# Two fp16 parts per operand in the tree layer's products, its weights loaded and split ahead

## The reference

```python
logits = x @ W_in.T + b_in                       # 2048 x 2040
decisions = (logits > 0).astype(jnp.int32).reshape(B, PAR, N_NODES)
acts = jax.nn.silu(logits).reshape(B, PAR, N_NODES)
...
for d in range(DEPTH):                           # 7 levels: walk from node to node by the decisions
    moves = jnp.take_along_axis(decisions, current[..., None], axis=2)[..., 0]
    current = (current - cur_platform) * 2 + moves + next_platform
    dmap = dmap + jax.nn.one_hot(current, N_NODES, dtype=acts.dtype)
masked = acts * jax.lax.stop_gradient(dmap)
out = masked.reshape(B, WIDTH) @ W_out.T         # 2048 x 256
```

## Time and profile before

| | us |
|---|---|
| median of 3 runs | 3735.11 |
| lowest and highest run | 3732.72, 3735.58 |
| profiled execution | 3734.91 |
| its span, first to last instruction | 3733.2 |
| PE busy in the span | 3208.2 (86%) |
| DVE busy in the span | 2112.1 (57%) |

### The profile page before, as it was taken

One profiled execution on the slowest core, in us unless ns is written; L12 is line 12 of the kernel. 1 busy time (PEld: TensorE's weight loads), 2 busy tenths in 40 slices (PEclk: granted clock), 3 DMA queues, 4 the chain that ended last, 5 costly groups with the idle time before them and its releaser, 6 DMA issues. The chain is left out here.

```text
span 3733.2 us, 108642 instructions
## 1 busy us (share of the span) xinstructions
PE 3208.2 (86%) x44394; PEld 2109.9 (57%) x44394; DVE 2112.1 (57%) x8196; ACT 1495.3 (40%) x4199; POOL 642.8 (17%) x361
## 2 busy tenths in 40 slices
PE   7798575898989895679984788899999999999899
PEld 3323342222323222578972334599999899999566
DVE  6312554555555533666648444377777777777554
ACT  3465542455555540477843122222222222222222
POOL 0000000466666671151210000000000000000000
PEclk8779787999999996789987899755555555555999
DMA  1000003000000004211120000100000000000000
GB/s 69 1 1 12 0 1 112 1 1 1 1 1 1 1 1 143 102 47 55 50 94 0 26 0 0 57 4 4 4 4 4 5 4 4 4 4 4 6 8 9
DMA packets 53375, 79.42 MB, mean 21 GB/s; under 512 B 11878, under 2 KB 43323, under 8 KB 51996
## 3 DMA queue, kind: packets, MB, share of 16 engines
q1 hardware_dynamic: 47504, 61.59, 5.0%
q0 software_dynamic: 3408, 9.34, 0.7%
q10 hardware_dynamic: 1988, 1.77, 0.2%
HBM read 56.01 MB, written 16.67 MB: 19 GB/s over the span
## 5 line engine op out<-in xcount | busy, mean ns | idle before, releaser
L1308 DVE TENSOR_REDUCE diff_mx<-diff_m_ps 128x1 f32<-128x512 f32 x512 | 329.9, 686 | 330.2 <-PE diff_m_ps L1158 330.2
L2773 PE MATMUL gru_sums<-gru_take,gru_u 128*128 128x4 f16 x12288 | 479.8, 167 | 4.4 <-issue 3.7
L2773 PE MATMUL gru_sums<-gru_keep,gru_u 128*128 128x4 f16 x12288 | 471.3, 166 | 1.3
L2773 PEld LDWEIGHTS gru_sums<-gru_take,gru_u 128*128 128x128 f16 x12288 | 432.8, 105 | 4.7 <-issue 3.7
L2773 PEld LDWEIGHTS gru_sums<-gru_keep,gru_u 128*128 128x128 f16 x12288 | 410.8, 104 | 14.8 <-issue 1.5
L1262 ACT ACTIVATE diff_probs<-diff_s_ps 128x512 f32<-128x512 f32 x512 | 277.9, 595 | 225.0 <-PE diff_s_ps L1152 225.0
L1152 PE MATMUL diff_s_ps<-diff_qk 32*128 32x512 f32 x1024 | 294.9, 649 | 63.7 <-DVE diff_mx L1308 56.1
L2773 PE MATMUL gru_sums<-gru_rh,gru_u 128*128 128x4 f16 x6144 | 279.6, 170 | 27.5 <-DVE gru_rh L2842 4.6
L1158 PE MATMUL diff_m_ps<-diff_qk 32*128 32x512 f32 x1024 | 293.5, 650 | 6.4 <-DVE diff_mx L1308 6.4
L1354 POOL TENSOR_TENSOR diff_sums<-diff_sums,diff_probs 128x2048 f32<-128x2048 f32 x64 | 289.3, 4520 | 32.0 <-ACT diff_probs L1262 31.8
L2773 PEld LDWEIGHTS gru_sums<-gru_rh,gru_u 128*128 128x128 f16 x6144 | 237.3, 107 | 69.9 <-DVE gru_rh L2842 6.6
(11 more groups left out here) (486 smaller groups left out, 5660.1 us busy)
## 6 DMA issues: line engine op xcount, KB each, us to landing
moe_weights<-in_L_ffn_W SPq DMA_DIRECT2D x16, 1024.0 KB, 13.0
expert_slots<-diff_blank SPq DMA_DIRECT2D x1, 5031.0 KB, 21.1
stream_a<-expert_slots SPq DMA_DIRECT2D x39, 129.0 KB, 2.1
moe_weights<-in_L_cond_w_R SPq DMA_DIRECT2D x1, 4096.0 KB, 14.8
moe_both<-expert_pairs SPq DMA_DIRECT2D x4, 1024.0 KB, 9.6
stream_b<-in_x SPq DMA_DIRECT2D x4, 512.0 KB, 8.1
hyp_wf<-in_L_cond_w_f SPq DMA_DIRECT2D x2, 1024.0 KB, 8.5
stream_b<-in_xT SPq DMA_DIRECT2D x1, 2048.0 KB, 12.5
```

Source lines behind the costliest of these rows:

```text
L1308: dve.tensor_reduce(mx[:, i % 2, kt, at:at + 1], m_ps[:, m % 3, :], X_AXIS, ALU.max).then_inc(ph.maxes_ready, 1)
L2773: last = pe.matmul(sums[:, par, g, m * B:(m + 1) * B], part[:, g, c, m * P:(m + 1) * P], state[:, c * B:(c + 1) * B], start=False, stop=(l ...
```

## The change

Both products of the tree are formed from two fp16 parts per operand: a first part (the value, scaled, rounded to fp16) and a second (what is left, in fp16). Three products stand for one: first x first, second x first and first x second.

- `linear_attention` now issues the tree's three loads too, behind the recurrence's eleven, on SP in its first block. The recurrence's preparation issues none.
- The recurrence's preparation finds the largest entries of the tree's weights and bias on DVE (three reductions), turns and spreads them through PE between the matmul groups n = 11 and n = 13, and derives scales. ACT forms the first parts of the weights in four pieces of 128 x 2048, behind its copies n = 15 to 18; DVE forms the second parts.
- The multiplication of `hist` by 1/SCALE at the end of the recurrence is gone.
- In the tree POOL makes the states' first part (fp16), copies the residual, copies the states whole, and subtracts for the second part.
- PE forms the logits from 24 fp16 matmuls of 512 columns, and the result from 48 fp16 matmuls of 256 columns. Its order within a tile: transposes 0 and 1, product 0, transposes 2, product 1, transposes 3, products 2 and 3.
- ACT copies each group of transposes out as the first part, scaled (`turn_first`); DVE then forms the second part from the same bank of PSUM and from the first part, and only this frees the bank and lets PE multiply (`turn_read`). So DVE has four more instructions per tile, behind the multiplication by the path and ahead of the next tile's bias.

```diff
--- before.py
+++ after.py
@@ linear_attention, first block, SP
-                next_weights.load(sp, io)
+                for weights in next_weights:
+                    weights.load(sp, io)
@@ recurrence, preparation, PE
+                        if n == 11:
+                            pe.wait_ge(ph.tree_found, 1)
+                            pe.transpose(pst[0:3, 6, 2 * P:3 * P], found[:, :], ident[:, :]).then_inc(ph.tree_turned, 1)
+                        if n == 13:
+                            pe.wait_ge(ph.tree_reduced, 1)
+                            pe.matmul(pst[:, 6, 3 * P:3 * P + 3], ones[0:3, :], spread[:, 1:4], start=True, stop=True
+                                      ).then_inc(ph.tree_spread, 1)
@@ recurrence, preparation, DVE
+                    dve.wait_ge(tree.loaded, 48)
+                    for k, (raw, _, _, _) in enumerate(layers):
+                        dve.tensor_reduce(found[:, k:k + 1], raw, X_AXIS, ALU.max, apply_absolute_value=True)
+                    dve.tensor_reduce(found[:, 2:3], tree.bin[:, :], X_AXIS, ALU.max, apply_absolute_value=True
+                                      ).then_inc(ph.tree_found, 1)
...
+                    for i, (k, at) in enumerate(HALVES):
+                        raw, first, second, gain_of = layers[k]
+                        dve.wait_ge(ph.tree_first, i + 1)
+                        dve.scalar_tensor_tensor(out=second[:, at], in0=raw[:, at], scalar=gain_of, in1=first[:, at],
+                                                 op0=ALU.mult, op1=ALU.subtract)
@@ recurrence, preparation, ACT
+                        if 15 <= n < 15 + len(HALVES):
...
+                            act.activation(first[:, at], raw[:, at], ACT.Copy, scale=gain_of).then_inc(ph.tree_first, 1)
@@ recurrence, end, DVE
-                dve.tensor_scalar(hist[:, :, :], hist[:, :, :], 1 / SCALE, None, ALU.mult)
@@ tree_block, PE
-                        for c in range(DC):
-                            last = pe.matmul(l_ps[:, g, :], tile[:, par, 0, c, :], win[:, c, g * 512:(g + 1) * 512],
-                                             start=(c == 0), stop=(c == DC - 1))
+                        for i, (px, pw) in enumerate(PRODUCTS):
+                            for c in range(DC):
+                                last = pe.matmul(l_ps[:, g, :], states[:, par, px, c, :], win[:, pw, c, g * 512:(g + 1) * 512],
+                                                 start=(i == 0 and c == 0), stop=(i == 2 and c == DC - 1))
...
+                    def multiply(g):
+                        pe.wait_ge(ph.turn_read, 4 * n + (g + 2))
+                        for j in range(4 * g, 4 * g + 4):
+                            for i, (pm, pw) in enumerate(PRODUCTS):
+                                pe.matmul(y_ps[:, par % 2, 0:D], mT[:, pm, j, :], wout[:, pw, j, :], start=(j == 0 and i == 0),
+                                          stop=False, skip_group_check=True)
@@ tree_block, POOL
-                    pool.tensor_copy(tile[:, par, 0, :, :], hist[:, :, at])
-                    pool.tensor_copy(tile[:, par, 1, :, :], x4T[:, :, at]).then_inc(ph.tile_copied, 1)
+                    pool.tensor_copy(states[:, par, 0, :, :], hist[:, :, at]).then_inc(ph.first_copied, 1)
+                    pool.tensor_copy(tile[:, par, :, :], x4T[:, :, at])
+                    pool.tensor_copy(whole[:, par % 2, :, :], hist[:, :, at]).then_inc(ph.first_copied, 1)
+                    pool.wait_ge(ph.first_copied, 2 * n + 2)
+                    pool.tensor_tensor(states[:, par, 1, :, :], whole[:, par % 2, :, :], states[:, par, 0, :, :], ALU.subtract
+                                       ).then_inc(ph.tile_copied, 1)
@@ tree_block, DVE (the bias becomes a multiply and add with parts.undo_in)
+                    for g in range(4):
+                        dve.wait_ge(ph.turn_first, 4 * n + (g + 1))
+                        dve.scalar_tensor_tensor(out=mT[:, 1, 4 * g:4 * g + 4, :], in0=t_ps[:, g % 2, :].rearrange("p (a b) -> p a b", b=P),
+                                                 scalar=parts.gain_acts, in1=mT[:, 0, 4 * g:4 * g + 4, :], op0=ALU.mult, op1=ALU.subtract
+                                                 ).then_inc(ph.turn_read, 1)
@@ tree_block, ACT
-                        act.copy(mT[:, 4 * g:4 * g + 4, :], t_ps[:, g % 2, :].rearrange("p (a b) -> p a b", b=P)
-                                 ).then_inc(ph.turn_read, 1)
+                        act.activation(mT[:, 0, 4 * g:4 * g + 4, :], t_ps[:, g % 2, :].rearrange("p (a b) -> p a b", b=P), ACT.Copy,
+                                       scale=parts.gain_acts).then_inc(ph.turn_first, 1)
```

More of the change, by code:

```diff
@@ L2611, in load, with __init__ @@
         sp.dma_start(self.condT[:, :, :], io["condT"]).then_inc(self.loaded, 16)
+class TreeParts:
+    def __init__(self, nc, ctx):
+        sb = lambda name, shape, dt: ctx.enter_context(nc.sbuf_tensor("tree_" + name, shape, dt))
+        self.win = sb("win_parts", [P, 2, DC, WIDTH], F16)
+        self.wout = sb("wout_parts", [P, 2, WC, D], F16)
+        self.scales = sb("scales", [P, 8], F32)
+        self.kept = sb("kept", [P, P], F32)
+        (self.gain_in, self.gain_out, self.undo_in, self.bound, self.gain_acts, self.undo_out, self.spare, self.gain_all) = [
+            self.scales[:, k:k + 1] for k in range(8)]
 class TreeWeights(EarlyWeights):
@@ L2624, in load, with recurrence @@
         sp.dma_start(self.wout[:, :, :], io["L1_ffn_W_out_T"].rearrange("(c p) n -> p c n", p=P)).then_inc(self.loaded, 16)
-def recurrence(nc, K, io, early, next_weights, x4T, hist):
+def recurrence(nc, K, early, tree, tree_parts, x4T, hist):
     ident, ones = K
@@ L2676, in recurrence @@
             pst = inner.enter_context(nc.psum_tensor("gru_mix", [P, 8, 512], F32))
+            found = inner.enter_context(nc.sbuf_tensor("tree_found", [P, 3], F32))
+            spread = inner.enter_context(nc.sbuf_tensor("tree_spread", [3, 4], F32))
+            tree_tops = inner.enter_context(nc.sbuf_tensor("tree_tops", [P, 3], F32))
+            layers = [(a[:, :, :].rearrange("p c n -> p (c n)"), b[:, 0, :, :].rearrange("p c n -> p (c n)"),
+                       b[:, 1, :, :].rearrange("p c n -> p (c n)"), gain_in)
+                      for a, b, gain_in in ((tree.win, tree_parts.win, tree_parts.gain_in), (tree.wout, tree_parts.wout, tree_parts.gain_out))]
+            HALVES = [(k, slice(lo, lo + WIDTH)) for k in range(2) for lo in (0, WIDTH)]
             with nc.Block() as block:
-                @block.sync
-                def _(sp):
-                    next_weights.load(sp, io)
                 @block.tensor
@@ L2878, with tree_block @@
 TILES_HELD = 4
-def tree_block(nc, K, early, x4T, hist, out):
-    ident, ones = K
+PRODUCTS = ((0, 0), (1, 0), (0, 1))
+def tree_block(nc, early, parts, ident, x4T, hist, out):
     with ExitStack() as ctx:
         ph = Phase(nc, ctx, "tree")
[L2886 to L2891, removed]
+        (ph.tile_copied, ph.first_copied, ph.logits_done, ph.biased, ph.dve_step, ph.silu_done, ph.masked,
+         ph.turned, ph.turn_first, ph.turn_read, ph.result, ph.stored, ph.out_read) = ph.semaphores(
+            "tile_copied", "first_copied", "logits_done", "biased", "dve_step", "silu_done", "masked", "turned",
+            "turn_first", "turn_read", "result", "stored", "out_read")
+        win, bin_, wout = parts.win, early.bin, parts.wout
+        states = ph.sb("states", [P, TILES_HELD, 2, DC, P], F16)
+        whole = ph.sb("whole", [P, 2, DC, P])
+        tile = ph.sb("tile", [P, TILES_HELD, DC, P])
         logits = ph.sb("logits", [P, TREES, NODES])
@@ L2936, in work, with turn @@
                     pe.wait_ge(ph.masked, n + 1)
-                    for g in range(4):
+                    def turn(g):
                         pe.wait_ge(ph.turn_read, 4 * n + max(g, 1))
@@ L3018, in work @@
                     act.wait_ge(ph.stored, 16 * n + 16)
-                    act.copy(res[:, par % 2, :], y_ps[:, par % 2, 0:D]).then_inc(ph.out_read, 1)
+                    act.activation(res[:, par % 2, :], y_ps[:, par % 2, 0:D], ACT.Copy, scale=parts.undo_out).then_inc(ph.out_read, 1)
                 act.sem_inc(ph.silu_done, 1)
@@ L3143, in whole_program @@
         tree, gru = TreeWeights(nc, ctx, tree_loaded), GruWeights(nc, ctx, gru_loaded)
-        linear_attention(nc, K, io, linear, gru, first, second)
-        recurrence(nc, K, io, gru, tree, first, states)
-        tree_block(nc, K, tree, first, second, out)
+        linear_attention(nc, K, io, linear, (gru, tree), first, second)
+        tree_parts = TreeParts(nc, ctx)
+        recurrence(nc, K, gru, tree, tree_parts, first, states)
+        tree_block(nc, tree, tree_parts, K[0], first, second, out)
 def kernel(**inputs):
```

50 lines of the change are left out of this document (39 added, 11 removed).

## The result

The changed kernel takes 3791.36 us (median of 4 runs, 3765.40 to 3801.05); beside it the kernel before took 3733.91. The ratio is 1.0157, with a 95% interval of 1.0104 to 1.021: some 57 us slower. The direction was forecast, the size was not: +20 was named, and the range ended at 3772.

What follows compares the result with a forecast made beforehand. PE was taken to bound the tree. Loop +14.2, first logits -2.2, tree's start +1.0, `hist` scaling -2.3, loads +1.5, preparation +0.3 give +12.5; with +8 for the clock, 3734.91 became 3755 us, range 3742 to 3772.

Steps and rivals of the forecast that it cites:

- the loop: Tree: wait cycle through DVE, PE and ACT, 17.0 us per tile where it was 16.48; cost +14.2 us.
- the clock: Tree: PE's waits let its granted clock fall for part of a tile, half a microsecond per tile, +8 us.
- the rival of the shorter loop: Tree: shorter ACT part and next bias starting early give a period of about 16.6 us, total 3741; chance 0.07.
- the 3.09 us: PE's work on the loop per tile: products of group 0, transposes of group 2, products of group 1.
- The rival with a fall in every tile: Tree: clock falls just ahead of the products, 1.5 us per tile, 23 us over 15 tiles, total 3770; chance 0.20.
- The upper bound of 46 us: Tree: the clock's largest cost, 3.09 us more in each of 15 tiles.
- 9.57 us from bias to transposes: Tree: DVE's time from a tile's bias until PE may transpose it, counted in every period.
- the scaling and the tree's start together: Before the tree's first logits: dropped scaling of `hist` -2.3 us, added copy and subtraction on POOL +1.0.
- first logits: Tree: first tile's logits, 8.65 us before, three passes instead of four, -2.2 us.
- the loads' place: Start of the linear attention: three more DMA issues on SP, about 0.5 us each, +1.5 us.
- the preparation: Recurrence's preparation: PE's two small extra instructions, +0.3 us; DVE's reductions end 3.9 us before PE reaches group 11.
- PE as the bound, and faster: Rival: with DVE's waits covered, tree tiles take PE's 13.0 us, total about 3680; chance 0.05.

Runs made afterwards that it cites:

- both fills and POOL later: Changed kernel plus useless PE products in both waits of each tile, POOL's copies waiting for the current tile's first transposes; 1.0037 of the kernel before.
- tuned order: Changed kernel reordered: second parts between next walk's steps, products 2 and 3 behind next tile's first transposes, POOL starting after the mask; 0.9858 of the kernel before.
- second layer only: Changed kernel with only the second layer in two fp16 parts, the first layer in fp32 as before; 1.0066 of the kernel before.

## Why the prediction was right or wrong

The 60.4 us of the 15 periods divide by these runs: 14.3 for the loop (255.2 - 240.9), 8.5 for POOL beside the walk (263.61 - 255.15), 37.6 for the clock (301.2 - 263.6).

- *The loop.* Right, in mechanism and size: 17.0 us were worked out, 17.01 stand where the clock is full and POOL elsewhere, and +14.2 became +14.3. Only half of it is the longer period: in the kernel before the second bias follows the first by 9.58 us, with both fills and POOL later by 17.11, and this first period alone is 7.5 of the 14.3. The forecast's sum had that in it without naming it. Its terms: ACT's part 0.687 (0.67), the second part 0.748 (0.75). The next bias does start 0.1 us before the last second part has ended, which the rival of the shorter loop had named; it takes that much off, no more. The rule of the Trainium skill that was weighed, VectorE: DVE Perf Modes, section on the TRN2 errata, would have made the second part 0.82 and the period 17.13, by an estimate; the trace goes against it here too.
- *The clock.* This is the step that failed: "A slow stretch begins somewhere in the tile and PE's dense work ends it, so I take half a microsecond per tile, +8". It costs 2.5 us per tile, 37.6. The stretch does not begin somewhere: it comes in nearly every tile and at the same place, behind the longer wait, at the end of the first transposes, and the loop's own products and transposes follow. Nor does PE's dense work end it soon: the 0.50 lasts 6.8 us, in which PE is busy for most (5.90 of 7.00 us in the row of 3627.50). So it covers all of the 3.09 us that the prediction had named as a bound: from the first product to the fourth transposes it is 3634.41 - 3628.60 = 5.81 us. The rival with a fall in every tile had the mechanism, and its 1.5 us, half of the 3.09, were too small for the same reason. The upper bound of 46 us was the nearer end, and the range should have reached it.
- *DVE's walk beside POOL.* Missed: 9.57 us from bias to transposes came from the last tile, in which POOL has no copies to make, and no term asked where those copies land once PE is early. They follow the tile's result, which used to come while DVE waited and now comes as the walk starts: 10.43. A rule of the Trainium skill bore on this and was not used: SBUF — State Buffer, Who interferes with whom, says that a VectorE instruction with two inputs from SBUF contends with a GpSimd instruction that reads SBUF, over a shared pair of ports. The runs agree in kind: small instructions with two SBUF operands got longer (128x32 from 195 to 541 ns), and recovered when POOL was moved.
- *Small terms.* Last copy of the states to first logits -0.95 (the scaling and the tree's start together, forecast -1.3); first logits -0.56 (-2.2), since 5.5 of their 8.09 us lie at half clock, where 3.0 of 8.65 did before; the loads' place +1.3 to +2.0 (+1.5); the preparation +0.65 (+0.3; its cover of 3.9 us held: in the timeline of the changed kernel, shown below, DVE's last reduction ends at 2374.29, and PE comes to its transposition at 2378.33 without a wait). ACT's last copy comes 2.4 us later behind the last bias than before (tail counted as unchanged), with the clock at 0.50 from 3781.03 to 3791.27. The rest of the 66.1, some 2.3 us, lies in the linear attention's loop and in other stretches, where single executions differ by as much.

```profile
2372.01 2.28 DVE L2775 TENSOR_REDUCE tree_found<-tree_bin 128x1 f32<-128x2048 f32 x1
...
2378.33 0.27 PE L2720 MATMUL gru_mix<-ident,tree_found 128*3 128x128 f32 x1
```

- *PE as the bound, and faster.* Rightly put as what would happen if DVE's waits were covered: the tuned order covers them, and takes 12.95 us per tile where 13.0 had been worked out, and 0.9858 of the kernel before where about 3680 of 3735 us, 0.985, had been named. The changed kernel's own program order does not.

## What to carry to other kernels

Shortening the busiest engine by adding steps to another one did not pay here, because the new steps closed a loop through both: add up such a loop first, then let the new steps of one tile lie beside the next tile's work. Where the new order makes TensorE wait in every iteration, price the case that the clock falls in every iteration, at the same place, over all the work that follows the wait, and check whether that work is on the loop. It does not have to fall: with waits of 0.4 and 1.1 us in a tile (second layer only) it held in the middle of the stage, with 2.6 and 1.1 it fell in nearly every tile. Durations taken from a first or last iteration leave out what a third engine does beside the others in the middle.

## What the runs showed of the hardware

- A slow stretch can lock to a loop: 0.50 for some 7 us of every 20.5, tile after tile, with 2.6 us of waiting ahead of the transposes at whose end it begins, and 1.1 us behind them. With one of the waits filled it came only every second or third tile, for 3.4 us; with both it did not come in the middle of the stage. So 2.5 us of useless products in each tile made the 15 periods 37.6 us shorter.
- Four of the six instructions of 128x8 to 128x32 elements in VectorE's walk took 0.11 to 0.35 us longer beside GpSimd's copies and subtraction, 0.7 us a tile; the bias addition, with one operand from PSUM, took 2.351 beside them (tuned kernel) against 2.341.
- It goes the other way too. In the kernel without second parts GpSimd's first copy, 0.40 us in the changed kernel, began within VectorE's multiplication by the path and took 1.93 us, until 0.26 us after that had ended:

```profile
3564.29 2.29 DVE L3075 TENSOR_TENSOR tree_acts<-tree_acts,tree_path 128x2048 f32<-128x2048 f32 x1 [0.22 <-ACT tree_acts L3086]
...
3564.91 1.93 POOL L3038 CAST tree_states<-stream_b 128x256 f16 x1 [9.76 <-PE tree_y_ps L3025]
```
